# One buffer of a Mamba block's B and C channels less, and the copies of them regrouped

## The chip, the cores and the metric

The kernel runs on one core of a Trainium2 chip. The metric is the device time of one launch in microseconds (us). Three runs of the kernel before gave 503.39, 503.79 and 505.11 us; the median is 503.79.

## The reference

The input is u of 2 batches x 2048 tokens x 128 channels. A first sublayer normalises it, projects it to z, x, B, C and dt, and runs a state-space scan in both directions of time over two heads:

```python
xBC = silu(causal_conv(xBC, conv_w, conv_b))      # 4 taps, 384 channels: x 256, B 64, C 64
h = h * exp(dt_t * A) + dt_t * x_t B_t^T          # per head: 128 x 64
y = h C_t + D * x_t
y = rmsnorm(y * silu(z)) * norm_w
u = u + ga * (y_forward + y_backward) @ out_proj_w.T
```

A second sublayer normalises again, picks one of 8 experts for each token (argmax of gate logits) and adds a two-layer ReLU network of that expert. All of it is float32.

## The kernel before

The scan is written in chunks of 128 tokens: 64 chunks Q in all (two batches, two directions of 16). Four chunks make a step S, so there are 16 steps, 0 to 15; j is the chunk's place in its step. Each of the five engines has its own stream written out by hand, and all order between engines is by semaphores. A stream never runs past an instruction that waits. After the scan comes a stage of 39 slots of 128 tokens for the experts (from about 376 us on); the change doesn't touch it.

The convolution of a step's 512 tokens is made one or two steps ahead. For B and C together (128 partitions: B in 0 to 63, C in 64 to 127) ACT writes the first tap to `accb` (`tap0_bc`, L899), POOL multiplies and adds the other three taps (`taps_bc`, L623 and L628), ACT takes a tanh of it to `bc` (`tanh_bc`, L917), and DVE forms (tanh + 1) * accb, which is the SiLU, in `cc` (`gate_bc`, L1629). Then ACT makes two copies of 64 partitions x 512: `keep_b` (L931) brings B to the lower half of `bb`, whose upper half was set to zero at the start (L1816), and `c_over_b` (L936) brings C over B in `cc`, so that C stands in both halves of `cc`. Both halves are wanted because DVE multiplies all 128 partitions of `cc` with the decays of the two heads (L1648 in `mix`). `tap0_bc` of the step after next stands between the two copies in ACT's stream, at j = 2 (`conv_first`). `gate_bc` of the next step stands at j = 1 in DVE's stream.

PE does two things for each chunk. `prepare(Q)` transposes x of two heads (L1223) and B (L1224), multiplies B with C (L1227), and makes the decays (L1229, L1230, L1234). `scan(Q)` makes state and output (L1249 to L1260). PE's stream is `prepare(Q+1)`, `scan(Q)`, and then side work (projections, output, gates). Before the first chunk of a step, `prepare` waits for the x of the step (`s_gx`) and for `c_over_b` (`s_cc`). ACT's stream in a chunk is: the squares of the last chunk, the copies of the transposes (L946, L948), the exponential of the decays (L957), the convolution's part, side work. DVE's is: `mix(Q+1)` (L1645, L1648), a convolution tap or gate, `carry` (L1660), `gate_y` (L1679), more taps, side work. POOL prepares the decays' left factor three chunks ahead (L664), does the taps of B and C, and small norms.

At the start of the launch DVE normalises four blocks of tokens (`stats`, L1497 and L1502, and `normed`, L1514). Before the statistics of the last of them it sets `bs`, `bb` and `st` (L1815 to L1817).

Of the kernel before, what the change touches and what calls it, by code (L numbers as in the profile page):

```python
# [11 lines left out]
ACT = mybir.ActivationFunctionType  # L12
AX_X = mybir.AxisListType.X

P = 128
B, L, DM = 2, 2048, 128
NH, HD, NS = 2, 128, 64
DI = NH * HD
# [5 lines left out]
BT = 4  # L24
BLK = BT * P
# [18 lines left out]
NSTEP = B * STEPS  # L44
# [14 lines left out]
def chunk_of(Q):  # L59

    b, q = divmod(Q, CHUNKS)
    return (b, 1, TPB - 1 - q) if q < TPB else (b, 0, q - TPB)
# [100 lines left out]
def build(nc, u, w_xbc, w_zdt, conv_w, conv_b, dt_bias, a_log, d_skip, norm_w, w_out, gate_w, gate_b,  # L163
          w1, w2, b2, c_t, wmod, out):
    ctx = ExitStack()
    with ctx:
        def sb(name, shape, dt=F32):
            return ctx.enter_context(nc.sbuf_tensor(name, shape, dt))

        def sem(name):  # L170
            return ctx.enter_context(nc.semaphore(name))
# [22 lines left out]
        ident = sb("ident", [P, P])  # L194
# [56 lines left out]
        accb = sb("accb", [P, BLK])  # L251
        prod = sb("prod", [P, BLK])
        cx = sb("cx", [P, 2, NH, BLK])
        bc = sb("bc", [P, BLK])
        bb = sb("bb", [P, 2, BLK])
        cc = sb("cc", [P, 2, BLK])
        cs = sb("cs", [P, 2, P])
        lseg = sb("lseg", [P, LA, NH, P])
# [82 lines left out]
        s_prod = sem("s_prod")  # L341
        s_thb = sem("s_thb")
        s_bc = sem("s_bc")
        s_bb = sem("s_bb")
        s_cc = sem("s_cc")

        s_L = sem("s_L")
        s_tx = sem("s_tx")
        s_sg = sem("s_sg")
# [3 lines left out]
        s_m = sem("s_m")  # L353
# [488 lines left out]
        def _(act):  # L842
# [41 lines left out]
            def decay_tables(b):  # L884

                u = USE["pfx", b]
                wait_full(act, u)
                act.activation(etab[:, b, :, :], side(u)[:, 0:2 * NQ].rearrange("p (k c) -> p k c", k=2), ACT.Exp)
                act.activation(etot[:, b, :, :],
                               side(u)[:, 2 * NQ:2 * NQ + 2 * TPB].rearrange("p (d t) -> p d t", d=2),  # L890
                               ACT.Exp).then_inc(free(u), 1)

            def tap0_bc(S):

                b, d, k = step_of(S)
                wait_free(act, USE["raw", NBLK * b + NBLK - 1 - k, 2])
                if S >= 1:
                    act.wait_ge(s_bc, S)
                act.activation(accb[:, :], raw[:, NH, at_raw(b, k):at_raw(b, k) + BLK], ACT.Identity,  # L899
                               bias=cb[:, d, NH:NG], scale=cw[:, d, NH, KC - 1:KC]).then_inc(s_tap0b, 1)  # L900

            def tap0_x(S, g):

                b, d, k = step_of(S)
                X = NH * S + g
                wait_free(act, USE["raw", NBLK * b + NBLK - 1 - k, g])
                if X >= 1:
                    act.wait_ge(s_gx, X)
                act.activation(bank[1][:, :], raw[:, g, at_raw(b, k):at_raw(b, k) + BLK], ACT.Identity,  # L909
                               bias=cb[:, d, g:g + 1], scale=cw[:, d, g, KC - 1:KC]).then_inc(s_tap0, 1)  # L910

            def tanh_bc(S):

                act.wait_ge(s_tapb, HALO * (S + 1))
                if S >= 1:
                    act.wait_ge(s_bc, S)
                act.activation(bc[:, :], accb[:, :], ACT.Tanh).then_inc(s_thb, 1)  # L917

            def tanh_x(S, g):

                if S >= 2:
                    act.wait_ge(s_sg, BT * (S - 1))
                act.wait_ge(s_tap, HALO * (NH * S + g + 1))
                act.activation(cx[:, S % 2, g, :], bank[1][:, :], ACT.Tanh).then_inc(s_th, 1)

            def keep_b(S):

                act.wait_ge(s_bc, S + 1)
                if S >= 2:
                    act.wait_ge(s_sg, BT * (S - 1))  # L930
                act.activation(bb[0:NS, S % 2, :], cc[0:NS, S % 2, :], ACT.Copy).then_inc(s_bb, 1)  # L931

            def c_over_b(S):

                act.wait_ge(s_bb, S + 1)
                act.activation(cc[0:NS, S % 2, :], cc[NS:2 * NS, S % 2, :], ACT.Copy).then_inc(s_cc, 1)  # L936

            def tokens_major(Q):

# [83 lines left out]
            softplus_log(0)  # L1023
            tap0_x(0, 1)
            tanh_bc(0)
            tanh_x(0, 1)
            decay_tables(0)
            keep_b(0)
            c_over_b(0)
            tap0_bc(1)  # L1030
            tap0_x(1, 0)
            tokens_major(0)
# [2 lines left out]
            def conv_first(S, j):  # L1035

                if S == 0 and j == 1:
                    tanh_x(1, 0)
                    tanh_bc(1)
                    tap0_x(1, 1)  # L1040
                elif S == 0 and j == 2:
                    tanh_x(1, 1)
                    keep_b(1)
                    tap0_bc(2)
                    c_over_b(1)
                    tap0_x(2, 0)
                elif j == 1:
                    if S + 1 < NSTEP:
                        tanh_x(S + 1, 1)
                        tanh_bc(S + 1)  # L1050
                    if S + 2 < NSTEP:
                        tap0_x(S + 2, 0)
                elif j == 2:
                    if S + 1 < NSTEP:
                        keep_b(S + 1)
                    if S + 2 < NSTEP:
                        tap0_bc(S + 2)
                    if S + 1 < NSTEP:
                        c_over_b(S + 1)
                elif j == 3 and S + 2 < NSTEP:  # L1060
                    tanh_x(S + 2, 0)
                    tap0_x(S + 2, 1)

            for Q in range(NCH):
                S, j = divmod(Q, BT)
# [5 lines left out]
                if Q + 1 < NCH:  # L1071
                    tokens_major(Q + 1)
                    decays(Q + 1)
                conv_first(S, j)
                if g is not None and j == 0:
                    forward(g)
# [67 lines left out]
        def _(pe):  # L1144
# [64 lines left out]
            def prepare(Q):  # L1209

                b, d, t = chunk_of(Q)
                S, j = divmod(Q, BT)
                c0 = (t % BT) * P
                tx, sg = bank[0], bank[2 + Q % 2]
                if j == 0:
                    pe.wait_ge(s_gx, NH * (S + 1))
                    pe.wait_ge(s_cc, S + 1)
                if Q % CHUNKS == 0:
                    pe.wait_ge(s_eparts, b + 1)
                if Q >= 1:  # L1220
                    pe.wait_ge(s_xt, Q)
                for h in range(NH):
                    pe.transpose(tx[:, h * HD:(h + 1) * HD], cx[:, S % 2, h, c0:c0 + P], ident[:, :])  # L1223
                pe.transpose(tx[:, DI:DI + P], bb[:, S % 2, c0:c0 + P], ident[:, :]).then_inc(s_tx, 1)  # L1224
                if Q >= 2:
                    pe.wait_ge(s_m, Q - 1)
                pe.matmul(sg[:, DI:DI + P], bb[:, S % 2, c0:c0 + P], cc[:, S % 2, c0:c0 + P],  # L1227
                          start=True, stop=True)
                pe.matmul(sg[:, DI + P:DI + 2 * P], pick[:, t, :], eparts[:, b, d, :], start=True, stop=True)  # L1229
                pe.matmul(sg[:, 0:DI], identb[:, :], negm[:, d, :, :].rearrange("p h i -> p (h i)"),  # L1230
                          start=True, stop=False, skip_group_check=True)
                pe.wait_ge(s_L, Q + 1)
                for h in range(NH):
                    last = pe.matmul(sg[:, h * P:(h + 1) * P], lseg[:, Q % LA, h, :], incl[:, d, :],  # L1234
                                     start=False, stop=True, skip_group_check=True)
                last.then_inc(s_sg, 1)
# [111 lines left out]
            pe.wait_ge(s_row, 1)  # L1348
            pe.wait_ge(s_scaled, 1)
            prepare(0)  # L1350
            for Q in range(NCH):
                S, j = divmod(Q, BT)
# [3 lines left out]
                if Q + 1 < NCH:  # L1356
                    prepare(Q + 1)
# [110 lines left out]
        def _(dve):  # L1468
# [155 lines left out]
            def gate_bc(S):  # L1624

                dve.wait_ge(s_thb, S + 1)
                if S >= 2:
                    dve.wait_ge(s_sg, BT * (S - 1))
                dve.scalar_tensor_tensor(out=cc[:, S % 2, :], in0=bc[:, :], scalar=1.0, in1=accb[:, :],  # L1629
                                         op0=ALU.add, op1=ALU.mult).then_inc(s_bc, 1)  # L1630

            def mix(Q):
# [180 lines left out]
            stats(2)  # L1813
            normed(2)
            dve.memset(bs[:, :, :, :, :], 0.0)  # L1815
            dve.memset(bb[NS:2 * NS, :, :], 0.0)  # L1816
            dve.memset(st[:, 0, :], 0.0)  # L1817
            stats(3)
            normed(3)
# [12 lines left out]
            softplus_end(0)  # L1832
            taps_x(0, 1)
            gate_bc(0)
            gate_x(0, 1)
            decay_copies(0)
# [49 lines left out]
            for Q in range(NCH):  # L1886
                S, j = divmod(Q, BT)
# [188 lines left out]
```

## Time and profile before

| | us |
|---|---|
| median of 3 runs | 503.79 |
| the profiled execution, its own time | 505.11 |
| its span, first to last instruction | 503.4 |
| PE, DVE, ACT, POOL busy | 400.3, 380.3, 273.1, 310.6 |
| mean granted TensorE clock | 0.883 |

All the rows come from this one profiled execution. Its own time is 1.7 us more than its span and 1.3 us more than the median. A busy share says how full an engine is and not what sets the end; for that the chain of waits is read. PE and PEld are matmuls and weight loads of the same engine. A float32 matmul appears as two records of each (the transposes as one).

### The profile page before, as it was taken

What the parts mean: (1) busy time and instruction counts of PE and PEld (TensorE: products, weight loads), DVE (VectorE), ACT (ScalarE), POOL (GpSimd) and SP (SyncE); (2) the same over time, 40 slices, a digit from 0 to 9 for tenths busy, and PEclk for the clock granted to TensorE, in tenths of its full rate; (3) what the DMA queues carried; (4) which work ended last, traced back from release to release, by engine and by line L of the source; (5) the groups of instructions that cost most, each with busy time, mean ns of one, the idle gap of its engine ahead of it and who ended that gap; (6) DMA issues with size and microseconds to landing.
All of it is one profiled execution on the core that took longest, in us unless ns stands there. A gap on an engine that the chain in (4) does not pass through costs nothing.

```text
span 503.4 us, 10274 instructions
## 1 busy us (share of the span) xinstructions
PE 400.3 (80%) x2890; PEld 358.2 (71%) x2890; DVE 380.3 (76%) x1148; ACT 273.1 (54%) x751; POOL 310.6 (62%) x468
## 2 busy tenths in 40 slices
PE   2784789798679879897999797789985239999991
PEld 1272677787569758686889697779884229999991
DVE  4667787999964978897888886789798507788772
ACT  2517378475545876585757656787741014444440
POOL 3580852644894557498979688558754604566562
PEclk9955799979776997999899988899996559999997
DMA  7200000000000000001010110001311367888750
GB/s 211 58 0 0 13 2 1 1 1 2 0 1 1 2 1 0 2 2 42 2 44 1 44 44 1 1 1 43 128 44 43 135 173 206 231 232 231 220 155 2
DMA packets 21559, 29.20 MB, mean 58 GB/s; under 512 B 4076, under 2 KB 14572, under 8 KB 21376
## 3 DMA queue, kind: packets, MB, share of 16 engines
q1 hardware_dynamic: 17808, 21.24, 15.2%
q0 software_dynamic: 2832, 6.50, 3.6%
q10 hardware_dynamic: 864, 0.80, 0.5%
q8 instruction: 25, 0.41, 0.4%
q14 instruction: 30, 0.25, 0.1%
HBM read 20.97 MB, written 8.01 MB: 58 GB/s over the span
## 4 chain that ended last, share of the span: by engine, by line
DVE 27%; PE 22%; issue 15%; POOL 11%; ACT 11%; DMA 6%; ACTq 1%; POOLq 0%; SPq 0%; DVEq 0%
DMA out_dram<-raw 5%; POOL out_dram L830 4%; DVE bank L1609 4%; DVE ms L1645 3%; DVE cx L1621 2%; PE bank L1162 2%; PE bank L1234 2%; ACT bs L948 2%; DVE yzf L1687 2%; DVE st L1660 2%; PE bank L1249 2%; ACT junk L971 2%; PE bank L1283 1%; PE bank L1252 1%; PE bank L1256 1%
## 5 line engine op out<-in xcount | busy, mean ns | idle before, releaser
L628 POOL TENSOR_TENSOR accb<-accb,prod 128x512 f32<-128x512 f32 x48 | 61.2, 1274 | 26.2 <-ACT accb L899 22.4
L1609 DVE SCALAR_TENSOR_TENSOR bank<-raw,cw,bank 128x512 f32<-128x512 f32 x96 | 71.9, 749 | 2.3 <-ACT bank L909 1.0
L1645 DVE SCALAR_TENSOR_TENSOR ms<-es,dtv,bank 128x128 f32<-128x128 f32 x128 | 38.5, 342 | 38.1 <-ACT es L957 37.3
L830 POOL DMA_INDIRECT out_dram<-raw x39 | 38.0, 975 | 34.7 <-DMA out_dram<-raw 14.3
L664 POOL TENSOR_SCALAR lseg<-strict,av 128x128 f32<-128x128 f32 x128 | 46.9, 378 | 6.5 <-PE bank L1234 5.4
L1223 PE MATMUL bank<-ident,cx 128*128 128x128 f32 x128 | 28.1, 304 | 21.0 <-ACT cc L936 8.3
L909 ACT ACTIVATE bank<-raw,cb,cw 128x512 f32<-128x512 f32 x32 | 25.0, 781 | 35.1 <-DVE cx L1621 35.0
L746 POOL DMA_INDIRECT routed_rows<-rows,rowat x32 | 32.1, 1005 | 19.2 <-issue 8.0
L1256 PE MATMUL bank<-xt,ms 128*128 128x128 f32 x256 | 41.0, 285 | 3.5 <-DVE cs L1648 3.5
L1234 PE MATMUL bank<-incl,lseg 128*128 128x128 f32 x256 | 43.5, 298 | 0.0
L1452 PE MATMUL bank<-raw 128*128 x312 | 43.1, 281 | 0.0
L1435 PE MATMUL bank<-raw,zs 128*128 128x128 f32 x312 | 42.9, 282 | 0.0
L1252 PE MATMUL bank<-xt,skip 128*128 128x128 f32 x256 | 42.0, 290 | 0.0
L1996 DVE TENSOR_SCALAR raw<-bank,zs 128x128 f32<-128x128 f32 x78 | 23.8, 346 | 22.6 <-PE bank L1435 22.5
L1122 ACT ACTIVATE raw<-bank 128x128 f32<-128x128 f32 x39 | 10.8, 277 | 55.3 <-PE bank L1424 53.4
L1223 PEld LDWEIGHTS bank<-ident,cx 128*128 128x128 f32 x128 | 17.5, 159 | 32.3 <-issue 23.3
L1260 PE MATMUL bank<-st,cs 128*128 128x256 f32 x128 | 39.7, 393 | 0.6 <-DVE st L1660 0.6
L1249 PE MATMUL bank<-xt,bs 128*128 128x128 f32 x240 | 39.9, 293 | 0.0
L623 POOL TENSOR_SCALAR prod<-raw,cw 128x512 f32<-128x512 f32 x48 | 34.1, 710 | 9.1 <-ACT raw L863 8.2
L1435 PEld LDWEIGHTS bank<-raw,zs 128*128 128x128 f32 x312 | 39.6, 199 | 0.0
L1256 PEld LDWEIGHTS bank<-xt,ms 128*128 128x128 f32 x256 | 35.8, 202 | 3.9 <-DVE cs L1648 3.9
L1452 PEld LDWEIGHTS bank<-raw 128*128 128x128 f32 x312 | 38.0, 192 | 0.5
(229 smaller groups left out, 1152.3 us busy)
## 6 DMA issues: line engine op xcount, KB each, us to landing
zs<-in_w_dram SPq DMA_DIRECT2D x39, 258.0 KB, 3.2
zs<-routed_rows SPq DMA_DIRECT2D x39, 130.0 KB, 2.8
xs<-in_u_dram SPq DMA_DIRECT2D x4, 512.0 KB, 5.2
raw<-in_w_dram SPq DMA_DIRECT2D x1, 2048.0 KB, 8.3
routed_rows<-padrow ACTq DMA_DIRECT2D x6, 130.0 KB, 2.7
out_dram<-raw POOLq DMA_INDIRECT x39
routed_rows<-rows,rowat POOLq DMA_INDIRECT x32, 2.6
yzb<-in_wmod_dram SPq DMA_DIRECT2D x1, 384.0 KB, 4.3
```

The source lines that it names most:

```text
L628: pool.tensor_tensor(accb[:, :], accb[:, :], prod[:, :], ALU.add).then_inc(s_tapb, 1)
L664: last = pool.tensor_scalar(lseg[:, Q % LA, h, :], strict[:, d, :], av[:, b, col(d, h, t)], 1.0, ALU.mult, ALU.mult)
L830: pool.indirect_dma_start(out_rows, bass.IndirectOffsetOnAxis(ap=tok[:, s % 4, :].bitcast(mybir.dt.uint32), axis=0), ob[:, s % 4, :], None ...
L1223: pe.transpose(tx[:, h * HD:(h + 1) * HD], cx[:, S % 2, h, c0:c0 + P], ident[:, :])
L1234: last = pe.matmul(sg[:, h * P:(h + 1) * P], lseg[:, Q % LA, h, :], incl[:, d, :], start=False, stop=True, skip_group_check=True)
L1249: pe.matmul(sn[:, h * HD:(h + 1) * HD], bs[:, Q % TM, h].rearrange("p g n -> p (g n)"), xt[:, Q % TM, h * HD:(h + 1) * HD], start=True, st ...
L1252: pe.matmul(ys[:, h * HD:(h + 1) * HD], skip[:, d * NH + h, :], xt[:, Q % TM, h * HD:(h + 1) * HD], start=(h == 0), stop=False, skip_group ...
L1256: pe.matmul(ys[:, h * HD:(h + 1) * HD], ms[:, Q % 2, h, :], xt[:, Q % TM, h * HD:(h + 1) * HD], start=False, stop=False, skip_group_check= ...
L1435: mm = pe.matmul(bank[2 + 2 * (s % 2) + f // 2][:, c0:c0 + P], w1b[:, s % RW, f * P:(f + 1) * P], hTs[:, s % 2, :], start=True, stop=True)
L1452: last = pe.matmul(y, hr[:, s % 2, f * P:(f + 1) * P], w2s[:, bass.ds(e, 1), f, :].rearrange("p a c -> p (a c)"), start=False, stop=(f == ...
L1609: dve.scalar_tensor_tensor(out=bank[1][:, :], in0=raw[:, g, c0:c0 + BLK], scalar=cw[:, d, g, k:k + 1], in1=bank[1][:, :], op0=ALU.mult, op ...
L1645: dve.scalar_tensor_tensor(out=ms[:, Q % 2, h, :], in0=es[:, Q % 2, h, :], scalar=dtv[:, b, col(d, h, t)], in1=sg[:, DI:DI + P], op0=ALU.m ...
```

## The change

`bc` gets two slots, and `gate_bc` writes its result back into `bc` and no longer into `cc`. B stays where it is, in partitions 0 to 63 of `bc`, so `bb`, its setting to zero and `keep_b` go. ACT makes two copies of C, one to each half of `cc`, one directly after the other (`two_c`), and `tap0_bc` comes behind both. PE transposes and multiplies only the 64 partitions of B. Two waits move: the wait for PE's reads of the slot goes from DVE's `gate_bc` to ACT's `tanh_bc`, and `two_c` waits for `s_m`, DVE's last read of the `cc` slot.

```diff
-        bc = sb("bc", [P, BLK])
-        bb = sb("bb", [P, 2, BLK])
+        bc = sb("bc", [P, 2, BLK])
...
             def tanh_bc(S):
+                if S >= 2:
+                    act.wait_ge(s_sg, BT * (S - 1))
                 act.wait_ge(s_tapb, HALO * (S + 1))
-                if S >= 1:
-                    act.wait_ge(s_bc, S)
-                act.activation(bc[:, :], accb[:, :], ACT.Tanh).then_inc(s_thb, 1)
+                act.activation(bc[:, S % 2, :], accb[:, :], ACT.Tanh).then_inc(s_thb, 1)
...
-            def keep_b(S):
+            def two_c(S):
                 act.wait_ge(s_bc, S + 1)
                 if S >= 2:
-                    act.wait_ge(s_sg, BT * (S - 1))
-                act.activation(bb[0:NS, S % 2, :], cc[0:NS, S % 2, :], ACT.Copy).then_inc(s_bb, 1)
-
-            def c_over_b(S):
-                act.wait_ge(s_bb, S + 1)
-                act.activation(cc[0:NS, S % 2, :], cc[NS:2 * NS, S % 2, :], ACT.Copy).then_inc(s_cc, 1)
+                    act.wait_ge(s_m, BT * (S - 1))
+                act.activation(cc[0:NS, S % 2, :], bc[NS:2 * NS, S % 2, :], ACT.Copy)
+                act.activation(cc[NS:2 * NS, S % 2, :], bc[NS:2 * NS, S % 2, :], ACT.Copy).then_inc(s_cc, 1)
...
                 elif j == 2:
                     if S + 1 < NSTEP:
-                        keep_b(S + 1)
+                        two_c(S + 1)
                     if S + 2 < NSTEP:
                         tap0_bc(S + 2)
-                    if S + 1 < NSTEP:
-                        c_over_b(S + 1)
...
-                pe.transpose(tx[:, DI:DI + P], bb[:, S % 2, c0:c0 + P], ident[:, :]).then_inc(s_tx, 1)
+                pe.transpose(tx[:, DI:DI + NS], bc[0:NS, S % 2, c0:c0 + P], ident[0:NS, 0:NS]).then_inc(s_tx, 1)
...
-                pe.matmul(sg[:, DI:DI + P], bb[:, S % 2, c0:c0 + P], cc[:, S % 2, c0:c0 + P],
+                pe.matmul(sg[:, DI:DI + P], bc[0:NS, S % 2, c0:c0 + P], cc[0:NS, S % 2, c0:c0 + P],
                           start=True, stop=True)
...
             def gate_bc(S):
                 dve.wait_ge(s_thb, S + 1)
-                if S >= 2:
-                    dve.wait_ge(s_sg, BT * (S - 1))
-                dve.scalar_tensor_tensor(out=cc[:, S % 2, :], in0=bc[:, :], scalar=1.0, in1=accb[:, :],
+                dve.scalar_tensor_tensor(out=bc[:, S % 2, :], in0=bc[:, S % 2, :], scalar=1.0, in1=accb[:, :],
                                          op0=ALU.add, op1=ALU.mult).then_inc(s_bc, 1)
...
             dve.memset(bs[:, :, :, :, :], 0.0)
-            dve.memset(bb[NS:2 * NS, :, :], 0.0)
             dve.memset(st[:, 0, :], 0.0)
```

The order at steps 0 and 1 changes in the same way.

## Rows read from the trace of the kernel before

**Rows 1.** The page: busy time, and the chain's share by engine.
```profile
PE 400.3 (80%) x2890; PEld 358.2 (71%) x2890; DVE 380.3 (76%) x1148; ACT 273.1 (54%) x751; POOL 310.6 (62%) x468
...
DVE 27%; PE 22%; issue 15%; POOL 11%; ACT 11%; DMA 6%; ACTq 1%; POOLq 0%; SPq 0%; DVEq 0%
```

**Rows 2.** Groups by line: busy us, mean ns | idle us before them, releaser.
```profile
L1223 PE MATMUL bank<-ident,cx 128*128 128x128 f32 x128 | 28.1, 304 | 21.0 <-ACT cc L936 8.3 <-issue 4.4 <-DVE eparts L1598 4.1
...
L936 ACT ACTIVATE cc<-cc 64x512 f32<-64x512 f32 x16 | 10.1, 628 | 0.4
...
L931 ACT ACTIVATE bb<-cc 64x512 f32<-64x512 f32 x16 | 10.0, 627 | 0.0
```

**Rows 3.** Timeline of ACT before step 12: start, us, instruction.
```profile
304.52 0.62 ACT L931 ACTIVATE bb<-cc 64x512 f32<-64x512 f32 x1
305.05 0.81 ACT L899 ACTIVATE accb<-raw,cb,cw 128x512 f32<-128x512 f32 x1
305.88 0.63 ACT L936 ACTIVATE cc<-cc 64x512 f32<-64x512 f32 x1
```

**Rows 4.** Timeline of PE there and before step 13: [idle before, releaser].
```profile
306.61 0.65 PE L1223 MATMUL bank<-ident,cx 128*128 128x128 f32 x2 [2.71 <-ACT cc L936]
...
322.54 0.41 PE L1223 MATMUL bank<-ident,cx 128*128 128x128 f32 x2 [2.71 <-ACT cc L936]
```

**Rows 5.** The chain of waits, pieces at the starts of six steps: start, us.
```profile
70.18 0.06 ACT cc L936
...
199.69 0.23 ACT cc L936
...
305.88 0.64 ACT cc L936
...
321.82 0.64 ACT cc L936
...
338.50 0.54 issue
```

**Rows 6.** Timeline of DVE after step 12's start.
```profile
309.53 0.61 DVE L1645 SCALAR_TENSOR_TENSOR ms<-es,dtv,bank 128x128 f32<-128x128 f32 x2 [1.21 <-ACT es L957]
```

**Rows 7.** Timeline of DVE at the start of the launch.
```profile
20.89 0.91 DVE L1816 MEMSET bb<- 64x1024 f32 x1 [0.25 <-issue]
21.90 0.27 DVE L1817 MEMSET st<- 128x256 f32 x1
```

**Rows 8.** Timeline of POOL there.
```profile
23.34 0.20 POOL L584 TENSOR_SCALAR ve<-mv 128x4 f32<-128x4 f32 x1 [3.83 <-DVE mv L1502]
```

**Rows 9.** Stretches: PE, PEld, DVE, ACT, POOL busy (x instructions), granted clock, DMA.
```profile
306.70:309.90 3.20, 3.20 (x16) 3.13 (x17) 1.96 (x5) 2.10 (x7) 3.12 (x6) 0.50 0.00 0
...
323.80:327.00 3.20, 3.20 (x15) 3.11 (x15) 1.85 (x5) 1.92 (x5) 1.99 (x3) 0.50 0.00 0
```

**Rows 10.** Timeline of PE at the decay sums, granted clock 0.50 there.
```profile
45.56 0.62 PE L1173 MATMUL bank<-av,strict 128*128 128x32 f32 x2
46.11 0.40 PE L1176 MATMUL bank<-av,ones 128*64 128x16 f32 x4
```

**Rows 11.** The chain of waits: PE pieces that bear on matmul spacing.
```profile
28.93 6.96 PE bank L1162 x32
...
54.40 0.21 PE bank L1224
...
363.79 0.11 PE bank L1224
```

**Rows 12.** Waits: engine, waiting line <- releaser: us in total, times, longest.
```profile
POOL rt L674 <- ACT junk L971: 29.1, 8, 7.3
...
POOL accb L628 <- ACT accb L899: 22.4, 9, 3.8
```

**Rows 13.** Stretches, columns as in rows 9.
```profile
26.80:39.50 12.70, 11.29 (x42) 9.71 (x42) 7.27 (x15) 2.35 (x4) 9.03 (x14) 0.50 0.00 0
...
250.00:300.00 50.00, 46.13 (x353) 41.66 (x352) 42.23 (x117) 32.00 (x92) 40.21 (x57) 0.97 0.10 33
```

More of the change, by code:

```diff
@@ L343, in build @@
         s_bc = sem("s_bc")
-        s_bb = sem("s_bb")
         s_cc = sem("s_cc")
@@ L1027, in _ @@
             decay_tables(0)
-            keep_b(0)
-            c_over_b(0)
+            two_c(0)
             tap0_bc(1)
@@ L1042, in conv_first @@
                     tanh_x(1, 1)
-                    keep_b(1)
+                    two_c(1)
                     tap0_bc(2)
-                    c_over_b(1)
                     tap0_x(2, 0)
```

## The prediction

> **What bounds the kernel now.** The page comes first [rows 1]. PE is busy 80% and DVE 76%, and the chain that ended last gives DVE 27%, PE 22%, POOL 11%, ACT 11% and 15% to issue. No engine is the bound by itself. The time is the sum of handovers between them, so an edit is worth what it takes from a handover on the chain, and nothing where it only frees a busy engine. The second view is the groups by line [rows 2]. PE is idle 21.0 us before L1223, the first transpose of a chunk, and the largest named part of that, 8.3 us, ends with ACT's L936, the copy `c_over_b`. That is the instruction whose place the change moves. The third is the timeline where it happens [rows 3, 4]. Before step 12, ACT runs `keep_b` at 304.52, `tap0_bc` at 305.05 and `c_over_b` at 305.88, and PE, idle for 2.71 us, starts at 306.61, 0.10 us after that copy's end at 306.51. Before step 13 PE is idle for another 2.71 us. The fourth is the chain of waits [rows 5], which says where this matters: L936 lies on it whole before steps 12 and 13 (0.64 us each), a wait of 0.54 us that the profile calls issue ends at 339.04 when step 14's copy is done, and it lies on it briefly before steps 1, 6 and 7 (70.18 to 199.69, three pieces), where the chain goes on through ACT's own stream and not to PE. In the other steps the chain runs through DVE at that time.
>
> **Part 1, `tap0_bc` behind both copies.** The second copy now starts where `tap0_bc` started, one pitch of 0.53 us behind the first (305.05 - 304.52), and not at 305.88: `s_cc` comes 0.83 us earlier [rows 3]. Both copies stay 64 x 512, 0.63 us each. Before steps 12 and 13 the whole 0.83 is on the chain: 2 x 0.83 = 1.66 us. After 12 the next waiter is DVE's L1645, which had waited 1.21 us for ACT's exponential [rows 6], more than 0.83, so nothing on DVE takes the gain back there. Before step 14 only the 0.54 us of the wait can go, since PE's y transposes end at 338.50: 0.54 us. Before steps 1, 6 and 7 ACT runs the same three instructions, and the chain goes on to what follows them. Where an instruction follows without a dependence, the pitch is about 0.1 us under its duration (0.53 against 0.62), and where `c_over_b` followed `tap0_bc` it was not (0.83 against 0.81). One such seam goes for each step: 3 x 0.1 = 0.3 us. The bounds of part 1 are zero, if some other chain is always just behind, and 14 x 0.83 = 11.6 us, the 14 steps in which `tap0_bc` stood between. I take the chain's own count, 2.5 us.
>
> What it moves back is `tap0_bc`, by one copy's pitch, 0.53 us. POOL waits for it in 9 of 16 steps, 22.4 us in all, and what is behind it in POOL's stream are the decay factors, which run three chunks ahead, the taps, and the norms. POOL then waits 29.1 us in 8 places for ACT's squares [rows 12], so it has idle time to absorb 0.53 us before the next thing that others need. Cost zero; if that cover were gone, 9 x 0.53 = 4.8 us.
>
> **Part 2, the waits.** `tanh_bc` now waits for `s_sg` of the block before last. The `tanh_x` just ahead of it in ACT's stream waits for the same value, so it never blocks. Behind it would be the first taps and the squares. `two_c` waits for `s_m` of a chunk that DVE mixed more than a chunk earlier, a lower value than the exponential just ahead of it on ACT has waited for. DVE's gate loses a wait that had long passed. All zero. The gate writes in place with the same shape, zero.
>
> **Part 3, the memset.** The 0.91 us of L1816 are on DVE at 20.89, and the next instruction starts at 21.90 [rows 7], a pitch of 1.01 us. Behind it are the statistics of the fourth block, for which POOL waits 3.83 us [rows 8], and from POOL's power the chain runs on without a break (normalising, transposes, 32 small matmuls, z, softplus, decay rows) to the first chunk, whose B transpose stands at 54.40 [rows 11]. So 1.01 us, fully on the chain. Bounds: zero, if the second block of tokens or a constant of POOL comes last instead, and 1.01.
>
> **Part 4, PE on 64 partitions.** The moving side of B's transpose shrinks from 128 to 64 columns. That gives little, because the weights still have 128 columns: L1162 moves 2 columns for each 128 x 128 weights and still takes 6.96 / 32 = 0.22 us at half clock, what L1224 takes with 128 [rows 11]. The gain lies between zero and half of it (0.05 to 0.11 us for a chunk); I take zero. The other side of this edit is a switch of the array's shape. The only one in the trace is L1173 (128 x 128) to L1176 (64 columns): the two records of L1173 at 0.21 each would let L1176 start at 45.98 or 45.99, and it starts at 46.11 [rows 10], so 0.12 us are lost at half clock, and nothing of the kind can be seen on the way back. No row shows a 64-row shape. I bound it by zero and by two switches at 0.12 (half at full clock). L1224 is on the chain in 17 of 64 chunks, the first at 54.40 and the last at 363.79 [rows 11], 8 of them at 0.21 (half clock) and 9 at 0.11. One switch each: 8 x 0.12 + 9 x 0.06 = 1.5 us; two: 3.0. I take 1.5, as the nearest row has a price on one side.
>
> The Trainium skill says that changing the tiling mode drains TensorE (TensorEngine Tiling (Array Packing), Key Properties). By this rule both switches of a chunk would cost, and part 4 would be 3.0 in place of 1.5 us; the way into L1176 agrees with it by 0.12 us and the way out does not show it.
>
> **Part 5, the clock.** After each of the two idle stretches of 2.71 us PE was granted half clock for the next three microseconds or so [rows 9], with PE full. After the first the chain runs through PE from 306.61 until ACT's exponential, which starts 0.4 us ahead of the 309.53 at which DVE starts [rows 4, 6]: 2.5 us, at full clock half, so the drop costs 1.2 us. After the second it runs through PE for the 3.2 us of the stretch: 1.6 us. The idle stretches shrink to 1.9 us. Whether that saves the clock no row shows, so I count half: 1.4 us. Bounds 0 and 2.8.
>
> **The sum** is -1.0 (memset) - 2.5 (part 1) + 1.5 (part 4) - 1.4 (clock) = -3.4 us. Against the profiled execution it makes 505.11 - 3.4 = 501.7 us. The median of the runs lies 1.32 lower, 503.79 us, and so the forecast for a median is 500.4. Something within 0.3% (1.5 us) of 503.79 can't be told from no change.
>
> **Rivals.** *Absorbed.* The earlier `s_cc` is taken back within the same chunk by DVE, which has 76% of the time filled and is on the chain more than any engine. For it: in most steps the chain is on DVE when L936 ends. Against it: 1.21 us of DVE's waiting after step 12. Then only the memset and the seams stay: -1.3 + 1.5 = +0.2, 504.0 us. Chance 0.22. The delay of POOL by `tap0_bc` is a weaker form, -3.4 + 4.8 = +1.4, 505.2 us at its full price, and I give it 0.04.
>
> *Warm start.* PE is at half clock from 26.8 to 39.5 [rows 13], after a stretch almost without matmuls. With the work 1.0 us earlier the clock may stay, and the 6.96 us of L1162, alone on the chain, would be half, 3.5 us less. With both drops of part 5 gone as well: -3.4 - 1.4 - 3.5 = -8.3, 495.5 us. Against it: three gaps in front remain. Chance 0.1.
>
> *Slower.* The switch into and out of the 64-row shape in each of 64 chunks, 0.24 us at half and 0.12 at full clock, 0.176 us in the mix of the chain, would sit on PE's stream, and PE becomes the bound where it is busy 46.13 of 50 us [rows 13]. In the 17 chunks it costs 3.0, less than the 3.5 us that parts 1 and 3 bring. It makes the kernel slower by over 1.5 us once (3.5 + 1.5) / 0.176 = 28 chunks feel it. With 40 of 64 it would be +7.0 - 3.5 = 507.3 us, and with 64 it is 511.6. Against it: PE still has 8% idle in that stretch and more elsewhere, 0.3 us for each chunk at least, so most chunks take it from idle time. Chance 0.12.
>
> **Chances and range.** The forecast has 0.52 and by itself reaches from 497.5 to 503.3: -3.4 - 1.4 - 1.5 = -6.3 with both drops gone and no switch cost, and -0.5 with no drop gone and a second switch. The rivals have 0.22, 0.04, 0.1 and 0.12. Faster by over 0.3%: 0.52 + 0.1 and a little of the absorbed case, 0.63; within: 0.24; slower: 0.13. For 8 in 10 the range goes from 496.0, which leaves out the warm start, to 504.7, which takes in the absorbed case.
>
> **What would show it.** Part 1 is right if the two copies stand 0.53 us apart, `tap0_bc` follows, and PE's idle before L1223 put down to `cc` falls from 2.71 to about 1.9 us before steps 12 and 13. It is wrong if PE's start there comes earlier and the start of the next step doesn't. Part 3 is right if the first L1224 starts near 53.4 and not at 54.40. Part 4 shows in the distance from the B transpose to the next record: 0.11 at full clock means no switch, 0.17 or more means one; and in the distance from L1227 to L1229. Part 5 shows in the granted clock of the three microseconds after those starts. The prediction fails if L1224 with its neighbours takes over 0.2 us more in a chunk, or if POOL's norms come onto the chain behind `tap0_bc`.

## The result, and the profile after

The change makes the kernel slower. Four runs of it gave a median of 510.33 us (509.23 to 512.35) against 503.98 us for the kernel before; 17 more executions of it took 507.03 to 510.71 us, and the median of all 21 is 509.43. The ratio is 1.0106 with a 95% interval of 1.0077 to 1.0135, which is 5.3 us more where 3.4 less were forecast, and above the upper end of 504.7. All ratios here are taken over fast runs alone, and some differ from the ratio of the two medians by up to 0.4%.

The page after, busy time and the chain's share by engine, answers to [rows 1]:

```profile
PE 412.4 (81%) x2890; PEld 351.3 (69%) x2890; DVE 381.7 (75%) x1147; ACT 275.7 (54%) x751; POOL 313.2 (62%) x468
...
PE 30%; DVE 21%; issue 21%; ACT 11%; POOL 8%; DMA 1%; SPq 1%; ACTq 0%; POOLq 0%; DVEq 0%
```

PE runs the same 2890 matmul records and is busy 12 us longer. It now leads the chain, with 30% in place of 22%. The groups by line answer to [rows 2] and show what the change was written for:

```profile
L1213 PE MATMUL bank<-ident,cx 128*128 128x128 f32 x128 | 27.3, 298 | 15.9 <-ACT cc L930 5.8 <-DVE eparts L1588 4.1 <-ACT bs L942 3.5
```

PE's idle time before a chunk's first transpose fell from 21.0 to 15.9 us, and the part that ends with the copies of C from 8.3 to 5.8 us. So the wait was shortened as planned, and the time was lost elsewhere. The timeline of PE in one chunk at full clock shows where. First the kernel before (start, us, instruction):

```profile
61.36 0.38 PE L1223 MATMUL bank<-ident,cx 128*128 128x128 f32 x2
61.58 0.27 PE L1224 MATMUL bank<-ident,bb 128*128 128x128 f32 x1
61.69 0.39 PE L1227 MATMUL bank<-cc,bb 128*128 128x128 f32 x2
61.91 0.22 PE L1229 MATMUL bank<-eparts,pick 96*128 96x128 bf16 x1
```

and the same four in the changed kernel:

```profile
61.01 0.38 PE L1213 MATMUL bank<-ident,cx 128*128 128x128 f32 x2
61.32 0.27 PE L1214 MATMUL bank<-ident,bc 64*128 64x64 f32 x1
61.43 0.44 PE L1217 MATMUL bank<-cc,bc 64*128 64x128 f32 x2
61.80 0.23 PE L1219 MATMUL bank<-eparts,pick 96*128 96x128 bf16 x1
```

Durations are of little use on PE, since they overlap. The starts tell it. From the first transpose to the decay matmul it was 0.55 us and is 0.79 us. Of the 0.24 us, 0.09 lie ahead of B's transpose, where the shape changes from 128 to 64 rows, and 0.15 between the product's first record and the decay matmul (0.37 in place of 0.22). In the single records these 0.15 are 0.06 between the product's two records and 0.09 at the change back. At half clock the same stretch, before:

```profile
157.76 0.67 PE L1223 MATMUL bank<-ident,cx 128*128 128x128 f32 x2
158.22 0.42 PE L1224 MATMUL bank<-ident,bb 128*128 128x128 f32 x1
158.44 0.64 PE L1227 MATMUL bank<-cc,bb 128*128 128x128 f32 x2
158.86 0.31 PE L1229 MATMUL bank<-eparts,pick 96*128 96x128 bf16 x1
```

and after:

```profile
158.96 0.67 PE L1213 MATMUL bank<-ident,cx 128*128 128x128 f32 x2
159.56 0.37 PE L1214 MATMUL bank<-ident,bc 64*128 64x64 f32 x1
159.72 0.74 PE L1217 MATMUL bank<-cc,bc 64*128 64x128 f32 x2
160.39 0.29 PE L1219 MATMUL bank<-eparts,pick 96*128 96x128 bf16 x1
```

It was 1.10 us and is 1.43, 0.33 us more: 0.14 on the way in (0.60 in place of 0.46), 0.06 less for B's transpose itself (0.16 in place of 0.22), and 0.25 for the product and the way back (0.67 in place of 0.42). All 64 chunks pay, 56 of them 0.24 and 8 of them 0.33, about 16 us of PE's stream.

Not all of the loss is in the scan. In the two profiled executions the first chunk starts 1.29 us earlier than before (52.45 against 53.74 us), the time from the first chunk's start to the last chunk's is 3.0 us longer (317.1 against 314.1), and what follows the last chunk's start is 3.0 us longer too (138.6 against 135.6), although the change doesn't touch that stage.

### The profile page after: what moved, and what is told of

It is laid out like the page before. It is cut to its first block, busy times and chain, and to the rows that moved or that the text cites. A ratio compares the mean times of both kernels' runs of the same rounds, so it can differ in the third digit from the quotient of the medians.

```text
span 508.1 us, 10258 instructions
## 1 busy us (share of the span) xinstructions
PE 412.4 (81%) x2890; PEld 351.3 (69%) x2890; DVE 381.7 (75%) x1147; ACT 275.7 (54%) x751; POOL 313.2 (62%) x468
## 4 chain that ended last, share of the span: by engine, by line
PE 30%; DVE 21%; issue 21%; ACT 11%; POOL 8%; DMA 1%; SPq 1%; ACTq 0%; POOLq 0%; DVEq 0%
PE bank L1425 5%; PE bank L1442 5%; DVE bank L1599 4%; DVE ms L1633 3%; PE bank L1152 2%; DVE cx L1611 2%; PE bank L1224 2%; ACT bs L942 2%; ACT junk L965 2%; POOL routed_rows L744 2%; POOL out_dram L828 1%; PE bank L1239 1%; ACT es L951 1%; PE bank L1242 1%; DVE st L1648 1%
## 5 line engine op out<-in xcount | busy, mean ns | idle before, releaser
L662 POOL TENSOR_SCALAR lseg<-strict,av 128x128 f32<-128x128 f32 x128 | 48.9, 396 | 5.6 <-PE bank L1224 4.5
L1242 PE MATMUL bank<-xt,skip 128*128 128x128 f32 x256 | 40.9, 284 | 0.0
L1213 PE MATMUL bank<-ident,cx 128*128 128x128 f32 x128 | 27.3, 298 | 15.9 <-ACT cc L930 5.8
L1224 PEld LDWEIGHTS bank<-incl,lseg 128*128 128x128 f32 x256 | 37.4, 210 | 0.0
```

The lines of the kernel that those rows point to most:

```text
L662: last = pool.tensor_scalar(lseg[:, Q % LA, h, :], strict[:, d, :], av[:, b, col(d, h, t)], 1.0, ALU.mult, ALU.mult)
L1242: pe.matmul(ys[:, h * HD:(h + 1) * HD], skip[:, d * NH + h, :], xt[:, Q % TM, h * HD:(h + 1) * HD], start=(h == 0), stop=False, skip_group ...
```

## The experiments

Twelve runs of ten different kernels were made, in three sittings, each sitting on one chip with the kernel before beside them. Its medians there were 505.66 (e1 to e4), 504.46 (e5 to e8) and 504.79 us (e9 to e12), so kernels are compared by their ratio to it. A ratio times 503.98 us is what the expectations, which are in us, are held against. In this section "the theory" is that the change of the array's shape costs the time, and the first rival is that the new order on ACT does, through POOL's later taps.

### e1: PE's part alone

```diff
-                pe.transpose(tx[:, DI:DI + P], bb[:, S % 2, c0:c0 + P], ident[:, :]).then_inc(s_tx, 1)
+                pe.transpose(tx[:, DI:DI + NS], bb[0:NS, S % 2, c0:c0 + P], ident[0:NS, 0:NS]).then_inc(s_tx, 1)
...
-                pe.matmul(sg[:, DI:DI + P], bb[:, S % 2, c0:c0 + P], cc[:, S % 2, c0:c0 + P],
+                pe.matmul(sg[:, DI:DI + P], bb[0:NS, S % 2, c0:c0 + P], cc[0:NS, S % 2, c0:c0 + P],
```

> The kernel before with only PE's part of the change: B's transpose and the product with C run on 64 partitions of bb and cc; copies, their order and the memset stay. Theory (shape switch): the B transpose starts 0.20 us behind the x transpose at full clock in place of 0.11, and the decay start matmul 0.20 behind the product in place of 0.11, 0.24 us more in each chunk; the kernel gets slower than before by 8 to 12 us, to about 514, more than the whole change did. Rival (order of ACT): PE on 64 partitions is harmless for the time, it stays within 1.5 us of before, and the loss of the change comes from tap0_bc behind the copies.

Measured: 1.0093 of before (1.0063 to 1.0124), +4.7 us. PE's timeline in e1 has the same spacing as the changed kernel:

```profile
63.62 0.38 PE L1223 MATMUL bank<-ident,cx 128*128 128x128 f32 x2
63.94 0.27 PE L1224 MATMUL bank<-ident,bb 64*128 64x64 f32 x1
64.05 0.44 PE L1227 MATMUL bank<-cc,bb 64*128 64x128 f32 x2
64.42 0.23 PE L1229 MATMUL bank<-eparts,pick 96*128 96x128 bf16 x1
```

The two edited lines make the loss, with ACT's order and the memset untouched. The size, 4.7 us by the ratio (3.2 to 6.3), is below the 8 to 12 that I expected. It may be the low reading: the medians beside each other, 512.40 and 505.66, are 6.7 us apart.

### e2 and e3: the order alone, the memset alone

```diff
 # e2
                         keep_b(S + 1)
+                        c_over_b(S + 1)
                     if S + 2 < NSTEP:
                         tap0_bc(S + 2)
-                    if S + 1 < NSTEP:
-                        c_over_b(S + 1)
 # e3
-            dve.memset(bb[NS:2 * NS, :, :], 0.0)
...
             taps_x(0, 0)
+            dve.memset(bb[NS:2 * NS, :, :], 0.0)
```

> The kernel before with only the order of ACT changed: keep_b, c_over_b, tap0_bc. PE stays at 128 partitions. Theory: 2.5 us from the chain, up to 2.8 more from the clock after steps 12 and 13, and so 499 to 501.5 us. Rival (order of ACT): POOL's later taps come onto the chain, 503.8 plus 3 to 7 us. A third, absorbed: within 1 us of before.

> The kernel before with only the setting to zero of bb's upper half moved, from ahead of the fourth block's statistics to behind DVE's first three taps. Theory: the start to the first chunk is 1.0 to 1.3 us shorter, and so 502.6 us. Rival: the first chunk starts earlier and the end doesn't move, 503.8.

Measured: e2 0.9988 (0.9965 to 1.0011), and e3 0.9952 (0.9926 to 0.9978). The order alone is worth nothing that can be told, neither the gain of the theory (2.5 us would be a ratio of 0.995, outside the interval) nor the loss of the rival; the third case, within 1 us, came true. The memset alone is worth 2.4 us, more than twice the forecast. DVE's timeline in e3 says why, against [rows 7]:

```profile
20.16 0.48 DVE L1815 MEMSET bs<- 128x512 f32 x1
20.65 0.27 DVE L1816 MEMSET st<- 128x256 f32 x1
20.84 0.80 DVE L1497 BATCH_NORM_STATS2 stat<-xs 128x6 f32<-128x128 f32 x4
```

The memset of `st` starts 1.25 us earlier, 20.65 in place of 21.90. The 0.25 us of issue ahead of the memset of `bb` went with it. PE's first transpose then starts at 51.68 in place of 53.74 us, 2.06 earlier. Of the other 0.8 us, 0.7 are clock: PE's 32 small matmuls take 6.28 us here in place of 6.96 [rows 11], at a granted clock of 0.56 in place of 0.50.

```profile
27.54 6.28 PE L1162 MATMUL bank<-wz,hT 128*128 128x2 f32 x32 [0.96 <-ACT hT L854]
```

That part is not sure to come. In the profiled execution of the changed kernel the same matmuls take 6.96 us at 0.50, and its first chunk starts only 1.29 us earlier; in that of e8 below they take 4.21 us at 0.87, and the first chunk starts at 49.73, 4.0 us earlier.

### e4: order and memset, PE on 128 partitions

> The kernel before with both, the order keep_b, c_over_b, tap0_bc and the moved setting to zero. This is the change without PE's 64 partitions, and it computes the reference. Theory: the two gains add, 3.5 us and some clock, 498 to 500.5 us, and it beats both kernels. Rival (order of ACT): slower than before, 505 to 509.

Measured: 0.9930 (0.9897 to 0.9963), a profiled execution of 499.72 us. That is 500.5 us by the ratio, at the upper end of what I expected. It computes the reference and is faster than both kernels, but not clearly faster than e3.

### e5: the changed kernel with PE on 128 partitions

```diff
-                pe.transpose(tx[:, DI:DI + NS], bc[0:NS, S % 2, c0:c0 + P], ident[0:NS, 0:NS]).then_inc(s_tx, 1)
+                pe.transpose(tx[:, DI:DI + P], bc[:, S % 2, c0:c0 + P], ident[:, :]).then_inc(s_tx, 1)
...
-                pe.matmul(sg[:, DI:DI + P], bc[0:NS, S % 2, c0:c0 + P], cc[0:NS, S % 2, c0:c0 + P],
+                pe.matmul(sg[:, DI:DI + P], bc[:, S % 2, c0:c0 + P], cc[:, S % 2, c0:c0 + P],
```

> The changed kernel with PE back on 128 partitions for both B instructions. As bc's upper half holds C and so does cc's, the product is then B C plus C C, which is not the reference's; instruction shapes are those of the kernel before. Theory (shape switch): from B's neighbour to the decay start matmul 0.44 us at full clock again, and the time falls below the kernel before, 498 to 501 us. Rival (order of ACT, waits of tanh_bc and two_c): it stays at 508 to 511.

Measured: 0.9951 (0.9921 to 0.9980). With everything else of the change in place, PE's two lines are worth 1.0106 / 0.9951 = 1.0156, about 7.8 us (5.7 to 9.9 from the two intervals). This is the other end of e1, and together they leave no room for the rival as the cause: e5 stands where the memset alone stands (e3, 0.9952), so ACT's order, the moved waits, the gate in place and the two copies of C cost nothing that can be told together, as part 2 of the prediction had it for its share.

### e6 and e7: where the price sits, and twice the dose

e6 puts only the transpose back on 128 partitions. e7 keeps 64 for both and puts B's transpose ahead of the x transposes, so that the shape changes four times in a chunk:

```diff
+                pe.transpose(tx[:, DI:DI + NS], bc[0:NS, S % 2, c0:c0 + P], ident[0:NS, 0:NS])
                 for h in range(NH):
-                    pe.transpose(tx[:, h * HD:(h + 1) * HD], cx[:, S % 2, h, c0:c0 + P], ident[:, :])
-                pe.transpose(tx[:, DI:DI + NS], bc[0:NS, S % 2, c0:c0 + P], ident[0:NS, 0:NS]).then_inc(s_tx, 1)
+                    last = pe.transpose(tx[:, h * HD:(h + 1) * HD], cx[:, S % 2, h, c0:c0 + P], ident[:, :])
+                last.then_inc(s_tx, 1)
```

> The changed kernel with the transpose of B on 128 partitions (the copy reads B's 64 columns only) and the product on 64. Theory: a switch costs whenever the shape changes, so there are still two for each chunk, and the time stays within 1.5 us of the changed kernel, 509 to 511. Rival: the cost sits in the transpose of 64 partitions itself, and half or more of it goes, 503 to 507.

> The changed kernel with the B transpose ahead of the x transposes and so apart from the product: four switches of the shape for each chunk in place of two. Theory: 0.18 us more in each chunk at full clock, and 5 to 10 us more, 515 to 520 us. Rival: the price is one for the 64-row instructions and not for the switch, and the time stays at 510.

Measured: e6 1.0089 (1.0057 to 1.0122), e7 1.0236 (1.0181 to 1.0292). PE's timeline in e6:

```profile
329.68 0.27 PE L1214 MATMUL bank<-ident,bc 128*128 128x128 f32 x1
329.88 0.49 PE L1217 MATMUL bank<-cc,bc 64*128 64x128 f32 x2
330.30 0.23 PE L1219 MATMUL bank<-eparts,pick 96*128 96x128 bf16 x1
```

The gap has only moved: 0.20 us now lie between the transpose and the product, and the product to the decay matmul takes 0.42. From the first x transpose (329.46) to the decay matmul it is 0.84 us, 0.05 more than in the changed kernel, so one 64-row instruction is no cheaper than two. In e7 it comes at each edge:

```profile
61.94 0.28 PE L1212 MATMUL bank<-ident,bc 64*128 64x64 f32 x1
62.15 0.44 PE L1214 MATMUL bank<-ident,cx 128*128 128x128 f32 x2
62.51 0.48 PE L1218 MATMUL bank<-cc,bc 64*128 64x128 f32 x2
62.93 0.23 PE L1220 MATMUL bank<-eparts,pick 96*128 96x128 bf16 x1
```

0.99 us from the first of them to the decay matmul, with the same instructions in another order that took 0.79, and the first of them starts 0.10 us late behind the projection ahead of it (its last record starts at 61.41 and takes 0.43 up to the next). So the two extra switches cost about 0.3 us in a chunk, where I expected 0.18, and are worth 1.0236 / 1.0106 = 1.0129, or 6.5 us of time. The time rose with the number of switches (two in the change and in e6, four in e7), and not with the number of 64-row instructions. No kernel with e7's order of instructions on 128 rows was run, so what the order alone does is not known.

### e8: the changed kernel with the old order on ACT

```diff
                     if S + 1 < NSTEP:
                         two_c(S + 1)
                     if S + 2 < NSTEP:
                         tap0_bc(S + 2)
+                    if S + 1 < NSTEP:
+                        second_c(S + 1)
...
```

`second_c` is the second of the two copies, taken out of `two_c`; the order at steps 0 and 1 changes in the same way.

> The changed kernel with tap0_bc back between the two copies of C. Theory: the order was worth 2 to 4 us also in the changed kernel, 512.5 to 514.5 us. Rival (order of ACT costs): 504 to 508 us. A third, absorbed: 510.

Measured: 1.0158 (1.0130 to 1.0186), 0.5% above the changed kernel, 511.9 us by the ratio where I expected 512.5 or more. The intervals overlap, and its four executions spread from 505.74 to 513.61 us, so this speaks for the new order, not more. It does speak against the rival.

### e9: the 64-row group first

```diff
-                for h in range(NH):
-                    pe.transpose(tx[:, h * HD:(h + 1) * HD], cx[:, S % 2, h, c0:c0 + P], ident[:, :])
-                pe.transpose(tx[:, DI:DI + NS], bc[0:NS, S % 2, c0:c0 + P], ident[0:NS, 0:NS]).then_inc(s_tx, 1)
                 if Q >= 2:
                     pe.wait_ge(s_m, Q - 1)
                 pe.matmul(sg[:, DI:DI + P], bc[0:NS, S % 2, c0:c0 + P], cc[0:NS, S % 2, c0:c0 + P],
                           start=True, stop=True)
+                pe.transpose(tx[:, DI:DI + NS], bc[0:NS, S % 2, c0:c0 + P], ident[0:NS, 0:NS])
+                for h in range(NH):
+                    last = pe.transpose(tx[:, h * HD:(h + 1) * HD], cx[:, S % 2, h, c0:c0 + P], ident[:, :])
+                last.then_inc(s_tx, 1)
```

> The changed kernel with the two 64-partition instructions first in prepare (the product, then B's transpose) and the x transposes behind them: still two switches for each chunk, but the first falls where PE has just come from the scan or from a wait. Theory: a switch that falls into a wait of PE costs nothing, and PE waits before about a quarter of the chunks, so up to 2 us less than the changed kernel, 507 to 511. Rival: no place hides it, and the x transposes, which ACT waits for, come 0.4 us later in each chunk: 512 to 518.

Measured: 1.0047 (1.0014 to 1.0081), 0.6% under the changed kernel, 3.0 us, more than the 2 us of the theory and far from the rival. The intervals of the two kernels overlap. It is still slower than 128 partitions. PE's timeline in e9:

```profile
328.45 0.49 PE L1214 MATMUL bank<-cc,bc 64*128 64x128 f32 x2
328.77 0.22 PE L1216 MATMUL bank<-ident,bc 64*128 64x64 f32 x1
328.92 0.44 PE L1218 MATMUL bank<-ident,cx 128*128 128x128 f32 x2
329.19 0.22 PE L1220 MATMUL bank<-eparts,pick 96*128 96x128 bf16 x1
```

From the first of them to the decay matmul it is 0.74 us. Where PE doesn't wait, the way in isn't hidden: in the chunk at 61.09 us the group starts 0.09 us late behind the projection (whose last record starts at 60.57 and takes 0.43 up to the next). In the same chunk the two records of the x transposes, of 128 rows and directly behind a switch, start at 61.56 and 61.73, 0.17 us apart in place of 0.11.

### e10 to e12: half the dose, and the order once more

e10 takes e4 and uses 64 partitions in every second chunk (`k = NS if Q % 2 else P`). e11 is e4 and e12 is e3, beside it.

> The kernel of e4 (order and memset, PE at 128 partitions) with 64 partitions in every other chunk only, 32 of 64. Theory: the cost follows the number of switches, so about half of what lies between e4 and the changed kernel (0.993 and 1.0106 of before): 1.000 to 1.003 of before. Rival: the cost is a threshold of PE being the bound, and half a dose costs under 1 us: 0.993 to 0.995.

> The kernel of e4 once more, on the chip of e10 and e12, as their reference. Theory: 0.991 to 0.996 of before.

> The kernel of e3 once more, beside e11: the two differ by the order of ACT alone. Theory (order is worth its 2.5 us): e11 is 0.4 to 0.9% faster than this one, which stands at 0.995 to 0.998 of before. Rival (absorbed): the two are within 0.2%.

Measured: e10 0.9979 (0.9960 to 0.9999), e11 0.9964 (0.9936 to 0.9991), e12 0.9944 (0.9922 to 0.9966). e10 missed what the theory gave it, 1.000 to 1.003. Half the dose costs 0.15% over e11, its reference in the same sitting, and 0.5% over e4, where half of the change's price would be about 0.7%. Against e11 that half lies outside the intervals and the rival's "under 1 us" fits (0.8 us); against e4 it lies inside. So e10 speaks, weakly, against a price in time that is in proportion to the number of switches. The chain says why it need not be: in e10's trace B's transpose lies on it in 16 chunks, and only 7 of these are on 64 rows. e11 and e12 show no gain from ACT's order with PE on 128 partitions: 0.9964 against 0.9944, after 0.9930 against 0.9952 in the first pair. The two pairs point opposite ways, and the rival's 0.2% fits.

## Why the prediction was wrong, point by point

**Part 4 failed, and it alone turned the sign.** I took one switch at 0.12 us (half clock) and 0.06 (full) in the 17 chunks whose prepare is on the chain, 1.5 us. Measured are 0.33 and 0.24 us for a chunk. There were three errors of size. Both directions cost, while I took the way back as free. The place I read it from [rows 10] has it, if the records are taken one by one: L1176's records start in two pairs, at 46.11 and 46.24, and L1173 follows the second pair by 0.20 us and not by 0.13. The price falls by a third with the clock, from 0.14 us for the way in at half clock to 0.09 at full, where I halved 0.12. And the product's two records moved apart, by 0.06 us at full and 0.11 at half clock. Taking the gain in B's transpose as zero was right at full clock and 0.06 us too low at half.

The number of chunks was wrong as well. With the right price my count of 17 gives 8 x 0.33 + 9 x 0.24 = 4.8 us, and e1 measured 4.7 by the ratio, but part of that is luck. In e1's own trace B's transpose lies on the chain in 25 chunks, 7 at half clock, which gives 6.6 us and is nearer to its medians. With dearer chunks, more of them came onto the chain: 25, 26, 24, 20 and 29 in e1, e8, e9, e6 and e7, against 17 and 14 with 128 rows (before, e5). A count from the trace before can't see that. The changed kernel doesn't fit the pattern, with 16 chunks on the chain (7 x 0.33 + 9 x 0.24 = 4.5 us), against 7.8 us between it and e5. In their two profiled executions, 3.4 us of the difference lie between the first and the last chunk, and 3.1 behind it.

By the runs the sum is -2.4 (memset, e3) + 0 (order and its clock, e2) + 7.8 (PE's lines, against e5) = +5.4 us, where mine was -3.4. The *slower* rival had the mechanism, but it named 28 chunks as the point from which it decides, at 0.176 us a chunk and gains of 3.5 us. The price was 0.24 or more, and the gains were 2.4 us.

The Trainium skill says that a change of tiling mode drains TensorE (TensorEngine Tiling (Array Packing), Key Properties). The traces agree in both directions: 0.09 us each at full clock in the changed kernel. I weighed it as 3.0 us and gave it a low chance.

**Part 1 did nearly what it said, and the time did not follow.** Before step 12 ACT's timeline after answers to [rows 3]:

```profile
308.56 0.63 ACT L929 ACTIVATE cc<-bc 64x512 f32<-64x512 f32 x1
309.20 0.63 ACT L930 ACTIVATE cc<-bc 64x512 f32<-64x512 f32 x1
309.85 0.82 ACT L897 ACTIVATE accb<-raw,cb,cw 128x512 f32<-128x512 f32 x1
```

The copies stand 0.64 us apart and not 0.53, so `s_cc` comes 0.72 us earlier and not 0.83. PE's wait there answers to [rows 4]:

```profile
309.93 0.41 PE L1213 MATMUL bank<-ident,cx 128*128 128x128 f32 x2 [1.89 <-ACT cc L930]
...
324.75 0.41 PE L1213 MATMUL bank<-ident,cx 128*128 128x128 f32 x2 [1.89 <-ACT cc L930]
```

1.89 us in place of 2.71, as forecast. PE's starts, read from each trace as the time from the first transpose of one step to that of a later one, show gain and loss:

| us | steps 6 to 9 | steps 11 to 14 |
|---|---|---|
| old order, 128 rows (before, e3, e12) | 74.6, 74.5, 74.7 | 49.7, 49.7, 49.7 |
| new order, 128 rows (e2, e4, e11, e5) | 76.1, 74.7, 79.4, 77.4 | 47.2, 47.5, 48.2, 48.4 |
| 64 rows in every second chunk, new order (e10) | 74.7 | 47.2 |
| 64 rows, old order (e1, e8) | 75.8, 76.8 | 50.4, 49.9 |
| 64 rows, new order (the change) | 77.6 | 47.3 |

Steps 11 to 14 gained 1.3 to 2.5 us, about the 2.2 that the chain's pieces had said for them. Steps 6 to 9 gave back 0 to 4.9 us. Each number is from one execution. In e11, the worst of them, PE was at half clock in two stretches. First e11, then e12 (PE, PEld, DVE, ACT, POOL busy, granted clock, DMA):

```profile
207.95:211.20 3.25, 3.25 (x19) 3.19 (x17) 1.93 (x7) 2.31 (x8) 1.71 (x4) 0.50 0.00 0
238.70:245.40 6.70, 6.70 (x32) 6.55 (x32) 2.54 (x10) 3.43 (x10) 6.33 (x10) 0.50 0.01 2
```

```profile
207.95:211.20 3.25, 3.25 (x24) 2.72 (x22) 2.79 (x9) 2.68 (x10) 2.55 (x5) 1.00 0.00 0
238.70:245.40 6.70, 6.70 (x46) 6.07 (x46) 4.97 (x11) 5.11 (x15) 6.41 (x9) 0.88 0.01 2
```

Between them DVE's gate of step 8 took 1.57 us in e11, where it had taken 0.68 at the same point of the kernel before:

```profile
219.11 1.57 DVE L1628 SCALAR_TENSOR_TENSOR cc<-bc,accb 128x512 f32<-128x512 f32 x1
220.60 2.90 DVE L1686 SCALAR_TENSOR_TENSOR yzf<-yzb,rn,yzf 128x256 f32<-128x256 f32 x4
```

POOL ran a 128 x 512 addition or multiplication beside it (L715 at 218.85); beside the 0.68 us in the kernel before it ran four operations of 128 x 128 (L711). Whether that is what slows DVE was not tested. So the *absorbed* rival was right about this part's time, and not by the way it named: where steps 6 to 9 give back, it is in other steps, whose clock and overlaps shifted, and not in the same chunk's DVE.

**Part 2** (waits, gate in place) was right at zero, shown by e5.

**Part 3** was right in mechanism and too small: 2.06 us on the first chunk in e3 and 0.48% and 0.56% of the time (e3, e12), 2.4 to 2.8 us for 1.0. In the changed kernel B's first transpose stands on the chain at 53.11, in place of 54.40, near the 53.4 that I had said. I counted the pitch behind the memset and left out 0.25 us of issue ahead of it, and the clock. The clock is the *warm start* rival, in part: it came nearly in full in one execution (e8), a little in e3, and not in the profiled execution of the change.

**Part 5** came true where I looked. The stretches that answer to [rows 9], after the changed kernel's two waits, are at full clock:

```profile
310.00:313.20 3.20, 3.20 (x25) 2.64 (x26) 3.09 (x9) 2.73 (x8) 2.45 (x4) 1.00 0.00 0
...
324.80:328.00 3.20, 3.20 (x26) 2.81 (x27) 3.09 (x9) 2.76 (x8) 2.42 (x4) 1.00 0.00 0
```

But counting two places was not a forecast for the whole. For the profiled executions, the loop (from the first chunk's first transpose to the last chunk's), what of it is at half clock, summed over stretches of 1 us, and the rest of the span behind it are:

| us | loop | at half clock | rest |
|---|---|---|---|
| old order, 128 rows (before, e3, e12) | 314.1, 314.4, 314.9 | 51, 48, 52 | 135.6, 135.4, 136.0 |
| new order, 128 rows (e2, e4, e11, e5) | 309.0, 310.4, 315.1, 313.7 | 36, 37, 53, 44 | 138.9, 135.3, 135.6, 135.4 |
| half the chunks, new order (e10) | 311.2 | 34 | 137.5 |
| 64 rows, old order (e1, e8) | 318.6, 320.0 | 48, 53 | 139.3, 134.2 |
| 64 rows, new order (the change) | 317.1 | 39 | 138.6 |

The new order mostly has less half clock and a shorter loop, but these are single executions: e2's was the second fastest of its twelve and e11's the slowest of its twelve, and e4 and e11, the same kernel, are 5 us apart. What one place gains, another can lose in a way that one profile doesn't foretell. The rest of the span, which no edit touches, is 3 us longer in some executions than in others, with either number of rows and either order, and none of it was forecast.

**What stays open:** whether PE's two lines really cost more in the changed kernel (7.8 us by the ratios) than in e1 (4.7 by the ratio, 6.7 by the medians), whether the new order is worth anything with PE on 64 partitions (e8), and what makes the stage behind the scan 3 us longer in some executions. The cause of the loss, PE's two lines, is shown; what the array does during the 0.09 us is not.

## What to carry to other kernels

A matmul on fewer rows was not a cheaper matmul here, but for 0.06 us of B's transpose at half clock, and each change of the array's shape within a stream of 128-row matmuls cost 0.09 us or more at full clock and 0.14 at half (the way in), in both directions. If a half-height operand must be used, keep its instructions together or pad with zeros, as the kernel before did. Price such an edit by the whole stream it sits in as well as by the chunks on the chain of the trace before, since more of them came onto it once each was dearer. A handover on the chain that gets shorter in three of 16 steps is worth what the other 13 leave of it, and a one-time setup at the start, ahead of work that all wait for, was the surest gain here.

## What the hardware showed that was not expected

The distance between two float32 records of the product grew from 0.11 to 0.17 us in the changed kernel, where it has 64 rows behind a switch (columns and clock the same). The rows alone don't explain it: in e9 the x transposes, of 128 rows, stand 0.17 us apart directly behind a switch. The two switches of a chunk, with the product between them, cost 0.33 us at half clock and 0.24 at full, and the way in 0.14 and 0.09: a part of it does not scale with the granted clock. Moving a memset of 0.91 us shifted the next instruction by 1.25 us. The 32 small matmuls at the start took 6.96, 6.28 and 4.21 us in three executions (the change, e3, e8), as the granted clock over them was 0.50, 0.56 and 0.87.
